# Inverse square roots through one shared activation table in a twelve-stage decoder kernel

## The reference

```python
def _layernorm(x, axis=-1, eps=1e-05):
    m = jnp.mean(x, axis=axis, keepdims=True)
    v = jnp.var(x, axis=axis, keepdims=True)
    return (x - m) / jnp.sqrt(v + eps)

x = _layernorm(x + _L0_attn_ref(x, ...), axis=-1)      # causal attention
x = _layernorm(x + _L0_xattn_ref(x, ctx, ...), axis=-1) # two-way attention
x = _layernorm(x + _L0_ffn_ref(x, ...), axis=-1)       # two local-attention layers with a gated GELU
x = _layernorm(x + _L1_attn_ref(x, ...), axis=-1)      # Mamba scan
...
x = _layernorm(x + _L3_ffn_ref(x, ...), axis=-1)       # mixture of experts
```

## Time and profile before

| | |
|---|---|
| median of 3 runs | 1801.82 us (1800.94 to 1801.95) |
| the profiled execution's own time | 1798.09 us |
| its span, first to last instruction | 1796.3 us |
| mean granted TensorE clock, share of full | 0.875 |
| busy: PE, DVE, ACT, POOL | 1427.7, 1135.3, 729.2, 412.1 us |
| instructions | 25705 |

### The profile page before, as it was taken

How to read it: one execution, slowest core, us unless ns; L and a number is a source line. 1 busy time by engine, 2 the same in 40 slices (tenths; PEclk the granted TensorE clock), 3 DMA queues, 4 the chain that set the end, 5 groups by cost and what they waited for, 6 DMA issues and landing times.

```text
span 1796.3 us, 25705 instructions
## 1 busy us (share of the span) xinstructions
PE 1427.7 (79%) x8738; PEld 936.6 (52%) x8754; DVE 1135.3 (63%) x2697; ACT 729.2 (41%) x1855; POOL 412.1 (23%) x375
## 2 busy tenths in 40 slices
PE   7999756776777556675796638989899899989997
PEld 5777634554455422221464426655566666666664
DVE  5667566664676578888666876655555766654333
ACT  3444424544445445455253513532233444432222
POOL 2233003322323034357410024200100333320000
PEclk9999878998789766768797868979999899999999
DMA  8000000000000400000000000000000000000000
GB/s 326 1 0 1 1 0 1 0 0 1 1 0 0 186 3 1 0 0 0 1 2 1 0 1 1 1 1 0 0 1 2 1 1 1 1 1 1 1 0 12
DMA packets 4202, 24.76 MB, mean 14 GB/s; under 512 B 1168, under 2 KB 3216, under 8 KB 3472
## 3 DMA queue, kind: packets, MB, share of 16 engines
q1 hardware_dynamic: 4112, 23.59, 3.2%
HBM read 23.06 MB, written 0.52 MB: 13 GB/s over the span
## 4 chain that ended last, share of the span: by engine, by line
PE 38%; issue 29%; DVE 16%; POOL 10%; ACT 5%; DVEq 0%; POOLq 0%; DMA 0%; ACTq 0%; SPq 0%
POOL arena L749 6%; PE PS L1234 5%; PE PS L868 5%; PE PS L1219 4%; PE PS L1220 4%; PE PS L843 3%; ACT arena L982 2%; DVE arena L2253 2%; POOL arena L2875 2%; POOL arena L2862 1%; PE PS L832 1%; DVE arena L2244 1%; DVE arena L2200 1%; PE PS L1223 1%; PE PS L195 1%
## 5 line engine op out<-in xcount | busy, mean ns | idle before, releaser
L561 ACT ACTIVATE arena<-PS,arena 128x256 f32<-128x256 f32 (+1 forms) x256 | 112.3, 443 | 175.2 <-DVE arena L659 101.2
L749 POOL TENSOR_TENSOR arena<-arena 128x384 f32<-128x384 f32 (+1 forms) x128 | 119.6, 935 | 243.5 <-DVE arena L669 129.8
L385 PE MATMUL PS<-arena 128*128 128x256 f32 (+1 forms) x512 | 135.3, 367 | 8.3 <-DVE arena L630 4.3
L982 ACT ACTIVATE arena<-PS 128x1024 f32<-128x1024 f32 (+1 forms) x96 | 86.4, 900 | 128.7 <-PE PS L868 128.7
L1322 DVE TENSOR_TENSOR arena<-arena,PS 128x512 f32<-128x512 f32 x82 | 56.4, 688 | 117.1 <-ACT arena L1255 117.0
L2309 POOL TENSOR_TENSOR arena<-arena 128x512 f32<-128x512 f32 x64 | 103.8, 1643 | 90.7 <-DVE arena L2244 36.0
L1255 ACT ACTIVATE arena<-PS 128x512 f32<-128x512 f32 x82 | 49.0, 597 | 165.3 <-PE PS L1220 165.3
L1054 DVE TENSOR_REDUCE arena<-PS 128x4 f32<-128x1024 f32 (+1 forms) x96 | 98.2, 1066 | 28.3 <-PE PS L843 28.3
L2244 DVE TENSOR_TENSOR_SCAN arena<-arena 128x512 f32<-128x512 f32 x64 | 94.0, 1473 | 21.8 <-ACT arena L2141 14.4
L385 PEld LDWEIGHTS PS<-arena 128*128 128x128 f32 x512 | 82.1, 190 | 42.7 <-issue 20.3
L868 PE MATMUL PS<-arena 32*128 32x256 f32 (+1 forms) x768 | 97.0, 371 | 6.9 <-ACT arena L982 3.5
(11 more groups left out here) (423 smaller groups left out, 3318.6 us busy)
## 6 DMA issues: line engine op xcount, KB each, us to landing
w_last<-in_last SPq DMA_DIRECT2D x1, 8260.0 KB, 22.9
w_rest<-in_rest SPq DMA_DIRECT2D x1, 5898.5 KB, 35.5
w_last<-in_first SPq DMA_DIRECT2D x1, 4532.5 KB, 20.2
w_last<-in_first SPq DMA_DIRECT2D x1, 2176.0 KB, 9.2
X<-in_x SPq DMA_DIRECT2D x1, 512.0 KB, 4.5
CT<-in_ctxT SPq DMA_DIRECT2D x1, 512.0 KB, 9.8
out<-X SPq DMA_DIRECT2D x1, 512.0 KB, 3.2
w_consts<-in_consts SPq DMA_DIRECT2D x1, 373.0 KB, 3.2
```

The lines of the kernel that those rows point to most:

```text
L385: ins = pe.matmul(PS[:, h % 2, col:col + n], self.QZ[:, h, t * P:(t + 1) * P], keys[:, 0:n], start=True, stop=not masked, skip_group_check ...
L561: ins = a.activation(self.Pr[:, h % 4, col:col + n], PS[:, h % 2, col:col + n], ACT.Exp, bias=self.nm[:, h, t:t + 1], scale=1.0, accum_out ...
L749: g.tensor_tensor(p, p, self.ri[:, h, 0:n].unsqueeze(2).to_broadcast([P, n, w // n]), ALU.mult)\
L982: a.activation(self.PT[:, k:k + 2, :], PS[:, 4:6, 0:2 * n], ACT.Exp).then_inc(self.e_done.sem, 1)
```

## The change

Every Sqrt on ScalarE with a reciprocal on DVE behind it becomes a Ln and an Exp with scale -0.5 on ScalarE, the Exp reading what the Ln wrote and waiting for it; DVE then begins with the refinement. Both functions are in one set, LOGS, which also serves the softmax Exps. The set is loaded at the program's start; in the other places loads are now written by hand: LOGS ahead of the wait of the root behind Mamba, BitLinear and Experts, Silu behind the router's Exp and at BitLinear's head, Gelu ahead of the waits of the three Gelus and LOGS behind them. The rest of the code is as before, so where the table that is surely loaded doesn't hold a function, the build still adds a load.

```diff
+LOGS = "natural_log_exp_and_others"
...
     def tiles(self, v, g):
         c, (a, b) = self.c, self.groups[g]
-        v.wait_ge(self.sd_ready.sem, self.sd_ready.at(0, g + 1))
-        c.dve.link(v, v.reciprocal(c.rs[:, a:b], c.sd[:, a:b]))
+        v.wait_ge(self.rs_ready.sem, self.rs_ready.at(0, g + 1))
         refine(lambda ins: c.dve.link(v, ins), v, c.rs[:, a:b], c.mv[:, a:b, 1], EPS, c.rt[:, a:b])
...
     def root(self, a, g):
         c, (i, j) = self.c, self.groups[g]
+        if self.reload:
+            a.preload_act_table_set(LOGS)
         a.wait_ge(self.var_ready.sem, self.var_ready.at(0, g + 1))
-        a.activation(c.sd[:, i:j], c.mv[:, i:j, 1], ACT.Sqrt, bias=c.eps, scale=1.0)\
-            .then_inc(self.sd_ready.sem, 1)
+        c.act.link(a, a.activation(c.ln[:, i:j], c.mv[:, i:j, 1], ACT.Ln, bias=c.eps, scale=1.0))
+        a.activation(c.rs[:, i:j], c.ln[:, i:j], ACT.Exp, scale=-0.5).then_inc(self.rs_ready.sem, 1)
...
         a.activation(self.lg[:, :, 0:self.cols], self.lg[:, :, 0:self.cols], ACT.Exp).then_inc(self.exp_ready.sem, 1)
+        a.preload_act_table(ACT.Silu)
         with a.Fori(0, self.ITERS) as it:
...
+        a.preload_act_table(ACT.Silu)
         c.act.link(a, a.activation(self.tmp, self.w1, ACT.Abs, accum_out=self.ab[:, 0:1]))
...
         a.activation(self.A, self.alog, ACT.Exp).then_inc(self.a_ready.sem, 1)
         a.wait_ge(self.var_ready.sem, self.var_ready.at(0, 1))
-        a.activation(c.sd[:, :], c.mv[:, :, 1], ACT.Sqrt, bias=c.eps, scale=1.0).then_inc(self.sd_ready.sem, 1)
+        link(a.activation(c.ln[:, :], c.mv[:, :, 1], ACT.Ln, bias=c.eps, scale=1.0))
+        a.activation(c.rs[:, :], c.ln[:, :], ACT.Exp, scale=-0.5).then_inc(self.rs_ready.sem, 1)
...
         def norms(it, d):
             a.wait_ge(self.sum_ready.sem, self.sum_ready.at(it, 1, d))
-            a.activation(self.nrm, self.ssq, ACT.Sqrt).then_inc(self.nrm_ready.sem, 1)
+            k = 3 if d else 1
+            a.activation(self.nrm, self.ssq, ACT.Ln).then_inc(self.log_ready.sem, 1)
+            a.wait_ge(self.log_ready.sem, self.log_ready.at(it, k))
+            a.activation(self.inv, self.nrm, ACT.Exp, scale=-0.5).then_inc(self.root_ready.sem, 1)
...
             a.wait_ge(self.var_ready.sem, self.var_ready.at(it, 1))
-            a.activation(self.sd2, self.mv2.rearrange("p (t k) -> p t k", k=2)[:, :, 1], ACT.Sqrt, bias=c.eps, scale=1.0)\
-                .then_inc(self.sd_ready.sem, 1)
+            a.activation(self.sd2, self.mv2.rearrange("p (t k) -> p t k", k=2)[:, :, 1], ACT.Ln, bias=c.eps, scale=1.0)\
+                .then_inc(self.log_ready.sem, 1)
+            a.wait_ge(self.log_ready.sem, self.log_ready.at(it, 2))
+            a.activation(self.rs2, self.sd2, ACT.Exp, scale=-0.5).then_inc(self.rs_ready.sem, 1)
...
                 norms(it, 1)
+            a.preload_act_table(ACT.Gelu)
             for f, m in enumerate(self.HID):
...
                              scale=1.0).then_inc(self.g_ready.sem, 1)
+            a.preload_act_table_set(LOGS)
             if self.depth == 0:
...
         def inverses(it, d):
-            v.wait_ge(self.nrm_ready.sem, self.nrm_ready.at(it, 1, d))
-            link(v.reciprocal(self.inv, self.nrm))
+            v.wait_ge(self.root_ready.sem, self.root_ready.at(it, 1, d))
             refine(link, v, self.inv, self.ssq, 0.0, self.nrt)
...
             s.end = LayerEnd(c, s.z_ready, last=i == len(names) - 1, early=isinstance(s, (Attention, NarrowAttention)),
-                             counted=s.ITERS if isinstance(s, Experts) else 0)
+                             counted=s.ITERS if isinstance(s, Experts) else 0,
+                             reload=isinstance(s, (Mamba, BitLinear, Experts)))
```

More of the change, by code:

```diff
@@ L103, in __init__ @@
         self.mv = sb("mv", [P, T, 2])
-        self.sd = sb("sd", [P, T])
+        self.ln = sb("ln", [P, T])
         self.rs = sb("rs", [P, T])
@@ L137, with __init__ @@
 class LayerEnd:
-    def __init__(self, c, z_ready, last=False, early=False, counted=0):
-        self.c, self.z_ready, self.last = c, z_ready, last
+    def __init__(self, c, z_ready, last=False, early=False, counted=0, reload=False):
+        self.c, self.z_ready, self.last, self.reload = c, z_ready, last, reload
         self.groups = [(0, T - 2), (T - 2, T)] if early else [(0, T)]
@@ L149, in __init__ @@
         self.var_ready = c.sig("var_ready", len(self.groups), 1)
-        self.sd_ready = c.sig("sd_ready", len(self.groups), 1)
+        self.rs_ready = c.sig("rs_ready", len(self.groups), 1)
         self.x_tile = c.sig("x_tile", T, 1)
@@ L1947, in __init__ @@
         N = self.N
-        self.var_ready, self.sd_ready = s("var_ready", 1, 1), s("sd_ready", 1, 1)
+        self.var_ready, self.rs_ready = s("var_ready", 1, 1), s("rs_ready", 1, 1)
         self.xn_ready = s("xn_ready", T, 1)
@@ L2184, in vector @@
         ins.then_inc(self.var_ready.sem, 1)
-        v.wait_ge(self.sd_ready.sem, self.sd_ready.at(0, 1))
-        link(v.reciprocal(c.rs[:, :], c.sd[:, :]))
+        v.wait_ge(self.rs_ready.sem, self.rs_ready.at(0, 1))
         refine(link, v, c.rs[:, :], c.mv[:, :, 1], EPS, c.rt[:, :])
@@ L2363, in __init__ @@
         self.sum_ready = s("sum_ready", 1)
-        self.nrm_ready = s("nrm_ready", 1)
+        self.log_ready = s("log_ready", 2)
+        self.root_ready = s("root_ready", 1)
         self.inv_ready = s("inv_ready", 1)
@@ L2385, in __init__ @@
         self.var_ready = s("var_ready", 1)
-        self.sd_ready = s("sd_ready", 1)
+        self.rs_ready = s("rs_ready", 1)
         self.n_ready = s("n_ready", 1)
@@ L2810, in batch @@
                 rotate(it, 1, 2)
-            v.wait_ge(self.sd_ready.sem, self.sd_ready.at(it, 1))
-            link(v.reciprocal(self.rs2, self.sd2))
+            v.wait_ge(self.rs_ready.sem, self.rs_ready.at(it, 1))
             refine(link, v, self.rs2, self.mv2.rearrange("p (t k) -> p t k", k=2)[:, :, 1], EPS, c.rt[:, 0:2])
```

## The result

The changed kernel takes 1779.84 us (median of 4 runs) beside 1801.38 for the kernel before: ratio 0.9879, 95% interval 0.986 to 0.9899, a gain of 21.5 us where I had forecast 7.2.

A forecast was written before the change was run, and what follows sets the result against it. Stages run one behind the other with engines handing over short pieces (PE 38% of the chain, ACT 5%), so loads cost only where others wait for ScalarE. Terms summed to -7.2 us, giving a median of 1794.6; range 1789.5 to 1798.0.

The forecast's parts named there:

- FourTokenAttention's Exp: In FourTokenAttention, the Exp without its load comes within 0.1 us of DVE's last sum, -1.30 us.
- L2f's wait: First Experts: PE's wait for the first hidden product falls from 1.92 to about 0.6 us, -1.30.
- LocalLayer's head: Head of the second LocalLayer: refinement starts at 449.81 instead of 450.77 without the load, -0.96 us.
- Ln to refinement: Roots: 0.52 us instead of 0.65 for LocalLayer's norms; 0.57 at layer ends as before, worth 0.
- BitLinear's first batch: BitLinear: without the load the fourth Silu ends at 993.98 instead of 995.03, -1.05 us.
- covered loads: Loads ending inside other engines' work, as in TwoWay and NarrowAttention: removing them was costed at 0.
- L3f -0.30: Second Experts: PE is busy and waits only 0.30 us for the product, so removing the load gives -0.30.
- -0.91 and -1.14 of LocalLayer's batches: LocalLayer's batches: -0.91 us from faster norms in seven, -1.14 from variance reciprocals leaving DVE in six.
- Rival 3: Slower: earlier work in the touched stages falls at TensorE's 1.2 GHz more often; 1805.4 us, chance 0.03.
- Rival 1: Only loads count; saved reciprocals and faster norms are eaten by PE or POOL; 1796.7 us, chance 0.20.
- Rival 2: More of the 32 vanished loads are on the path than seen; 1790.7 us, chance 0.12.
- Rival 4: Loads come back when the set is chosen anew for each Exp; 1801.8 us, chance 0.02.

The follow-up runs named there:

- b_moved: Kernel before with only loads moved: Exp's ahead of the wait in FourTokenAttention and both Experts, Silu's to BitLinear's head; 1789.93 us, ratio 0.9938.
- a_vrecip: Changed kernel with one DVE reciprocal put back before the variance refinement in LocalLayer's eight batches; two executions at 1788.8 and 1790.1 us, two near 1825.
- a_covered: Changed kernel with 16 loads put back at LocalLayer's variance root, the attentions' early layer-end groups and NarrowAttention's head; ratio 0.9882 to the kernel before.
- b_pad1: Kernel before with one DVE memset of 512 columns added in the layer end behind L1a; 1800.57 us.
- b_pad2: Kernel before with two DVE memsets added in the layer end behind L1a; 1824.76 us.
- b_pad4: Kernel before with four DVE memsets added in the layer end behind L1a; 1806.22 us.
- a_pad4: Changed kernel with four DVE memsets added in the layer end behind L1a; 1802.89 us.
- b_nfill: Kernel before with two matmuls nobody reads put in TensorE's 1.12 us wait for NarrowAttention's first Exp; 1790.63 us, ratio 0.9942.
- a_nwait: Changed kernel with one 1.28 us load between the wait and the first Exp in each of three NarrowAttention stages; 1805.98 us, ratio 1.0036.

## Why the prediction was wrong

**The local terms came out where they can be read in place.** 40 loads; FourTokenAttention's Exp 0.11 behind the scores (1.29 put back); L2f's wait 0.62; LocalLayer's head -0.96; Ln to refinement 0.52 for the norms and 0.57 at layer ends; BitLinear's first batch: its last Silu ends 21.94 us into the stage instead of 22.98, -1.04 against -1.05; covered loads 0. One was off: L3f -0.30, the load put back cost 0.0. The -0.91 and -1.14 of LocalLayer's batches were not measured as times of the stage.

**The step that failed is the sum.** It took TensorE's time as fixed, so that a stage without an edit on its path was a stage without a gain. From L0f on the stages differ by -21.6 us in the two profiles. My sum had -7.2 in L0f, L1f, L2a, L2f and L3f; there the profiles show -3.9, -1.4, -1.6, -2.9 and -0.5, 10.3 together. The other 11.3 lie in L1a (-2.3), L1x (-3.5), L2x (-4.5), L3a (-1.4) and +0.4 in L3x, which I had at zero. That they come from the clock is shown: for L1x by filling one wait, for L2x by b_moved, where no edit stands in the stage and its step down is gone (-4.2), for L1a and L1x by a_vrecip, which has the change's code there and the lengths of before, and for L2f and L3a by a pure delay that gives -1.7 and -1.2 with no edit. For L0f it is likely: the time at 1.2 GHz there is 98.4 us before, 87.6 in the change, and 91.1 in the change's second profile, where the same code takes 353.9 instead of 350.5. Only in L1x is the deciding wait known; for the others none was tried.

**Rival 3 named the mechanism and had its sign and size wrong.** I wrote that nothing makes TensorE idler and so let the clock only take away, and gave it 0.03. I priced it by single groups of eight matmuls at 0.68 us each. It acts by stretches of a whole 10, 34 or 44 us in stages where PE is busy over 90% of the time, 4 or 15 to 19 us each. The row that would have told me was there: the clock row reads 7, 9, 7 over L1x and 8, 9, 7 over L2x, where PE is busy nearly throughout. I read it as a price and not as a lever.

The range was built on the same omission. A fair one would have asked what L1x and L2x are worth without their 1.2 GHz stretches (the rows above say 4 each) and with longer ones, and would have been some 15 us wide on either side. The size of the gain was not to be predicted from the profile of before; that it could be 7 plus or minus such amounts was.

**Rival 1** is open: the 2 us of the reciprocals and norms in L0f can't be told from the clock's, and a_vrecip speaks for it rather than against. **Rival 2** falls for the 16 loads of a_covered; no run put the other covered ones back (TwoWay, Mamba's head, the last Attention among them), but L3x did not get shorter, nor did L1a in a_vrecip, and L0x (69.6 us) lies between its two values of before (68.8 and 70.3). **Rival 4** is excluded by the 40 loads.

## What to carry to other kernels

Where TensorE fills a stage and the granted clock there is below 1, look for the last PE wait ahead of each step down, and price that wait at the stretch behind it, not at its own length: here 1.12 us was worth 4 to 19 us in L1x, and two matmuls that nobody reads removed the step. Before crediting an edit with a gain, put a pure delay of some tenths of a microsecond in the kernel and see how far its time jumps; here 0.36 us gave 23. And give the loads that a ScalarE chain waits for their own length, the covered ones nothing.

## What was not expected of the hardware

A step to 1.2 GHz can follow a single wait of 1.12 us, or even 0.61, with TensorE busy for over 90% of the stage. In L1x it stands at the same place, 14.3 to 14.4 us into the stage, in two executions of the kernel before and in b_pad1, b_moved and a_vrecip. The Trainium skill (TensorE: Matmul & The Clock Gate, A second HAM failure mode: psum-queue depth-cycling) says of another kernel that TensorE idles briefly between groups of matmuls so often that its clock goes back and forth between the two levels. The trace agrees that short waits can do it, but here the wait ahead of the step is one, not a series.

The step is not certain: the same wait in the change passed without one. What decides was not found, but the profiles narrow it. The start of L2x is covered by a stretch at 1.2 GHz that begins in the layer end before it. In the ten profiles in which L2x's unfilled wait of 1.12 us passes without a step (those with filled layer ends left out), this stretch begins 4.4 to 5.5 us before the stage; in the four with a step behind it (b_pad2, b_pad4, a_pad4, a_covered) it begins 5.7 to 5.8 us before. b_nfill, with the wait filled, has 5.8 and no step. So some tenths of a microsecond in where that earlier stretch lies go with the outcome; that they cause it is not shown.

The steps keep their place against the program when the input lands up to 4 us later, but not when a stage in the middle is delayed by 0.36 us. And the level that follows is not always short: 10.2 us in the kernel before, 34 us in L1x of a_nwait and 44 us in b_pad2, with PE busy throughout.
